# Four weights laid out transposed by the host, and rotary query weights split in attention (Trainium2, one core)

## The reference, cut to what matters

```
x  : 2048 x 512, normalised per row (xn)
q  = xn @ wq.T                  16 heads of 128 + 64 columns; rotary on the last 64
kv = xn @ wkv_a.T               128 latent columns + 64 rotary ones (rotary applied)
kv_cache = rmsnorm(kv_lat) * kv_norm_w
q_lat  = q_nope @ wkv_b[:, :128]          per head, 128 columns
scores = (q_lat . kv_cache + q_pe . k_pe) * 192**-0.5, causal, softmax
out    = ((attn @ kv_cache) @ wkv_b[:, 128:].T) @ wo.T
ffn    = xn @ ternary(w_ffn).T * mean|w_ffn| + b_ffn
result = x + out + ffn
```

## Time and profile before

| | us |
|---|---|
| median of 3 runs | 1843.85 |
| lowest and highest | 1839.24, 1846.14 |
| span of the profiled execution, first to last instruction | 1833.3 |
| preparation in it (to attention's first matmul) | 176.42 |
| busy: PE 1715.3 (94%), DVE 1211.6 (66%), POOL 1009.4 (55%), ACT 849.0 (46%) | |

### The profile page before, as it was taken

One profiled execution on the slowest core, in us unless ns is written; L12 is line 12 of the kernel. 1 busy time (PEld: TensorE's weight loads), 2 busy tenths in 40 slices (PEclk: granted clock), 3 DMA queues, 4 the chain that ended last, 5 costly groups with the idle time before them and its releaser, 6 DMA issues. The chain is left out here.

```text
span 1833.3 us, 28210 instructions
## 1 busy us (share of the span) xinstructions
PE 1715.3 (94%) x9326; PEld 1446.9 (79%) x9326; DVE 1211.6 (66%) x2801; ACT 849.0 (46%) x1358; POOL 1009.4 (55%) x635
## 2 busy tenths in 40 slices
PE   6999789888999999999999999989999999999996
PEld 5887577667777777778888888878888888888885
DVE  4765476656666776666676666767677666766763
ACT  4554344443444544444544445434544544554442
POOL 4674544443555555555556556554646555565654
PEclk9888899989999999999999999999999999999998
DMA  6995355563766656756555545565756565655553
GB/s 196 371 331 212 107 148 171 161 216 110 202 172 167 160 151 179 210 167 172 150 149 154 157 132 149 170 188 151 191 132 151 146 164 130 158 153 130 149 129 109
DMA packets 127680, 309.12 MB, mean 169 GB/s; under 512 B 29554, under 2 KB 42099, under 8 KB 126388
## 3 DMA queue, kind: packets, MB, share of 16 engines
q1 hardware_dynamic: 98784, 227.04, 43.7%
q10 hardware_dynamic: 28756, 80.35, 15.8%
HBM read 113.28 MB, written 34.60 MB: 81 GB/s over the span
## 5 line engine op out<-in xcount | busy, mean ns | idle before, releaser
L1416 POOL TENSOR_TENSOR pT<-pT,pT_h 128x1024 fp32r<-128x1024 f32 x320 | 689.3, 2184 | 415.2 <-ACT pT_h L1322 413.2
L1196 DVE TENSOR_SCALAR_CACHE_REDUCE probs<-p_score 128x512 f32<-128x512 f32 (+3 forms) x640 | 382.2, 603 | 371.7 <-PE p_score L1124 225.9
L1301 ACT ACTIVATE probs<-probs,neg_max 128x128 f32<-128x128 f32 (+15 forms) x256 | 307.6, 1202 | 449.7 <-DVE neg_max L1202 399.4
L1322 ACT ACTIVATE pT_h<-pT 128x1024 fp32r<-128x1024 f32 x320 | 291.2, 963 | 241.9 <-PE p_out L1144 175.1
L1218 DVE STREAM_TRANSPOSE turned<-probs 128x1024 f32<-128x1024 f32 (+7 forms) x384 | 341.8, 916 | 40.6 <-ACT probs L1301 36.1
L1144 PE MATMUL p_out<-pT_h,V_h 128*128 128x256 f32 (+3 forms) x1024 | 301.3, 294 | 22.7 <-POOL pT L1416 22.6
L1144 PE MATMUL p_out<-pT,V_h 128*128 128x256 f32 (+3 forms) x1024 | 303.2, 296 | 0.0
L1144 PE MATMUL p_out<-pT_h,V_l 128*128 128x256 f32 (+3 forms) x1024 | 302.8, 296 | 0.0
L1124 PE MATMUL p_score<-Kp,qp_h 128*128 128x512 f32 (+3 forms) x640 | 236.8, 370 | 16.8 <-POOL qp_l L1408 16.7
L1124 PE MATMUL p_score<-Kn_h,q_h 128*128 128x512 f32 (+3 forms) x640 | 241.2, 377 | 3.5 <-DVE q_l L1241 3.0
L1124 PE MATMUL p_score<-Kn_l,q_h 128*128 128x512 f32 (+3 forms) x640 | 234.5, 366 | 0.0
(11 more groups left out here) (135 smaller groups left out, 2348.4 us busy)
## 6 DMA issues: line engine op xcount, KB each, us to landing
pT<-turned SPq DMA_DIRECT2D x384, 128.0 KB, 3.5
Wq<-wq_scr ACTq DMA_DIRECT2D x63, 512.0 KB, 4.4
Wv<-wv_scr SPq DMA_DIRECT2D x63, 512.0 KB, 3.8
pT<-turned SPq DMA_DIRECT2D x192, 112.0 KB, 3.8
pT<-turned SPq DMA_DIRECT2D x192, 96.0 KB, 2.6
pT<-turned ACTq DMA_DIRECT2D x128, 128.0 KB, 3.9
Wp<-wp_scr SPq DMA_DIRECT2D x31, 512.0 KB, 4.8
pT<-turned SPq DMA_DIRECT2D x192, 80.0 KB, 2.8
```

The source lines that it names most:

```text
L1196: dve.tensor_scalar(probs[row % ROW_RING][:, b * CW:b * CW + width], p_score[n % SCORE_RING][:, 0:width], SCALE, LOWEST, ALU.mult, ALU.max ...
L1301: act.activation(probs[row % ROW_RING][:, 0:width], probs[row % ROW_RING][:, 0:width], ACT.Exp, bias=neg_max[p][:, i:i + 1], scale=1.0, ac ...
L1322: act.activation(high.rearrange("p r t i q -> p r t (i q)"), low.bitcast(F32).rearrange("p r t i q -> p r t (i q)"), ACT.Copy).then_inc(p_ ...
L1416: pool.tensor_tensor(low.rearrange("p r t i q -> p r t (i q)"), low.bitcast(F32).rearrange("p r t i q -> p r t (i q)"), high.bitcast(F32). ...
```

## The change

The host now hands over four weights transposed: `woT` (per head), `kvaT`, `ffnT`, and `wpT`, the rotary rows of wq for each pair of heads, reordered and transposed. In preparation, the transposes of wo, wkv_a and w_ffn, the order matmuls and the splitting and storing of rotary weights go. wo is split where it was loaded (ACT in `high_parts`, DVE in the new `low_outputs`, both inputs in SBUF). Of the four parts of `weights`, the query product moves from slot 2 to slot 0 of each head's four, with its results' copies from 2 to 1, the output product from 3 to 2. `norm(0)` on POOL goes ahead of `low_parts(0, 0)`, and x goes ahead of the other loads on SP. The ternary weights are written straight as ffnT. In attention, `wpT` is loaded raw (256 KB a pair), and ACT and POOL split it in the place right behind the split of the rotated queries (in the third chunk, in the other half of the head).

```diff
+def rotary_weights_unit(s):
+    if phase(s) == 2:
+        return 1 if closes_head(s) else None
+    return (2, 5, None, 6)[phase(s)] if opens_head(s) else None
...
@@ sync, prepare
-                sp.dma_start(wqp[ROPE * i:ROPE * (i + 1), :], wq_heads[h][NOPE:QK, :]).then_inc(s_load[i], 16)
-                sp.dma_start(wo[i][:, :, :], wo_heads[h]).then_inc(s_load[i], 16)
+                sp.dma_start(wo[i][:, :], t["woT"][h]).then_inc(s_load[i], 16)
+            sp.dma_start(x_in[:, :, :], x_chunks[NCH - 1]).then_inc(s_x, 16)
             sp.dma_start(ident[:, :], t["ident"]).then_inc(s_const, 16)
-            sp.dma_start(w_kva[:, :, :], t["wkv_a"].rearrange("(a p) i -> p a i", p=96)).then_inc(s_const, 16)
-            sp.dma_start(x_in[:, :, :], x_chunks[NCH - 1]).then_inc(s_x, 16)
+            sp.dma_start(kvaT[:, :, :], t["kvaT"]).then_inc(s_kva, 16)
...
+            sp.dma_start(keep["wp_raw"][:, :, :], t["wpT"][0]).then_inc(s_wp, 16)
...
-                    if k % 2:
-                        sp.wait_ge(s_pe_h, n + 1)
-                        sp.wait_ge(s_pe_l, n + 1)
-                        sp.dma_start(t["wp_scr"][...], Wp[:, :, :, :].bitcast(F32)).then_inc(s_wp_out, 16)
@@ gpsimd, prepare
-                pool.tensor_tensor(wqp_l[half, :], wqp[half, :], wqp_h[half, :].bitcast(F32),
-                                   ALU.subtract).then_inc(s_low, 1)
...
+            norm(0)
             low_parts(0, 0)
-            norm(0)
...
+                    if first and s == 15:
+                        pool.wait_ge(s_wp_h, 1)
+                        pool.tensor_tensor(Wp[:, 1, :, :], keep["wp_raw"][:, :, :], Wp[:, 0, :, :].bitcast(F32),
+                                           ALU.subtract)
@@ scalar, prepare
-                act.activation(wqp_h[half, :], wqp[half, :], ACT.Copy).then_inc(s_high, 1)
                 act.activation(wqn_h[i][:, :], wqn[i][:, :], ACT.Copy).then_inc(s_high, 1)
+                act.activation(woT_h[i][:, :], wo[i][:, :], ACT.Copy).then_inc(s_high, 1)
...
+            def low_outputs(c, k):
+                n, i = QB * c + k, k % 2
+                dve.wait_ge(s_high, 3 * n + 3)
+                dve.tensor_tensor(woT_l[i][:, :], wo[i][:, :], woT_h[i][:, :].bitcast(F32),
+                                  ALU.subtract).then_inc(s_woT_l, 1)
...
+                    if s % 4 == 2 and (more or s < 12):
+                        low_outputs(c, s // 4 + 1)
@@ attention
-                sp.wait_ge(rot_projected, g // 2)
-                sp.dma_start(Wp[:, :, :, :].bitcast(F32), t["wp_scr"][g % H // 2]).then_inc(wp_in, 16)
+                need(sp, wp_low, g // 2 - 1)
+                sp.dma_start(wp_raw[:, :, :], t["wpT"][g % H // 2]).then_inc(wp_in, 16)
...
-                need(pe, wp_in, 16 * (g // 2))
+                need(pe, wp_low, g // 2)
...
+            def high_rotary_weights(g):
+                act.wait_ge(wp_in, 16 * (g // 2))
+                act.wait_ge(rot_projected, g // 2)
+                act.activation(Wp[:, 0, :, :], wp_raw[:, :, :], ACT.Copy).then_inc(wp_high, 1)
...
+            def low_rotary_weights(g):
+                pool.wait_ge(wp_high, g // 2)
+                need(pool, qp_ready, issued["rotary"])
+                pool.tensor_tensor(Wp[:, 1, :, :], wp_raw[:, :, :], Wp[:, 0, :, :].bitcast(F32),
+                                   ALU.subtract).then_inc(wp_low, 1)
```

More of the change, by code:

```diff
@@ L606, in round_ @@
                         square(c, (4, 5, 7, 9).index(s))
-                    if first and s in LINEAR_SLOTS:
-                        for it in LINEAR_SLOTS[s]:
-                            copy_linear(it)
                     if s in (6, 8, 10, 11):
@@ L616, in round_ @@
                         high_parts(c, s // 4 + 1)
+                    if first and s == 15:
+                        act.wait_ge(s_wp, 16)
+                        act.activation(Wp[:, 0, :, :], keep["wp_raw"][:, :, :], ACT.Copy).then_inc(s_wp_h, 1)
             rounds(ENG.Activation, round_)
@@ L819, in weights @@
                 if part == 0:
[L821 removed]
+                    pe.wait_ge(s_low, 2 * n + 2)
                     need(pe, s_q_l, n)
[L823 to L839 removed]
                     for it in range(IT):
@@ L1390, in _ @@
         def _(pool):
-            issued = {"low": 0, "rotary": 0}
+            issued = {"low": 0, "rotary": 0, "weights": 0}
             def add_rotary(g):
@@ L1403, in low_rotary @@
                 need(pool, p_low, issued["low"])
+                need(pool, wp_low, issued["weights"])
                 need(pool, qp_ready, issued["rotary"])
@@ L1483, in constants @@
     by_chunk = lambda a: np.ascontiguousarray(a.T.reshape(P, NCH, CW).transpose(1, 0, 2))
-    order = np.zeros((2, ROPE, ROPE), np.float32)
-    for x in range(2):
-        for f in range(HALF):
-            order[:, 2 * f + x, HALF * x + f] = 1.0
     return {
@@ L1495, in constants, with transposed @@
         "sinT": by_chunk(np.concatenate([sin, -sin, sin, -sin], 1)),
+    }
+def transposed(wo, wkv_a, w_ffn, wq):
+    by_input = lambda w: np.ascontiguousarray(w.T.reshape(IT, P, -1).transpose(1, 0, 2))
+    apart = np.concatenate([np.arange(0, ROPE, 2), np.arange(1, ROPE, 2)])
+    pairs = wq.reshape(H // 2, 2, QK, D)[:, :, NOPE + apart, :].reshape(H // 2, P, D)
+    return {
+        "woT": np.ascontiguousarray(wo.T.reshape(H, VDIM, D)),
+        "kvaT": by_input(wkv_a[np.concatenate([np.arange(RANK), RANK + apart])]),
+        "ffnT": by_input(w_ffn),
+        "wpT": np.stack([by_input(w) for w in pairs]),
     }
@@ L1508 @@
     arrays["x"] = arrays["x"].reshape(S, D)
+    arrays.update(transposed(arrays.pop("wo"), arrays.pop("wkv_a"), arrays.pop("w_ffn"), arrays["wq"]))
     arrays.update(constants())
```

175 lines of the change are left out of this document (49 added, 126 removed).

## The result

| | before | after |
|---|---|---|
| median of 20 runs each, us | 1843.61 | 1850.59 |
| lowest and highest, us | 1832.57, 1849.12 | 1842.51, 1862.00 |
| profiled execution: span, mean granted clock | 1833.3, 0.976 | 1851.1, 0.967 |

The ratio of the times is 1.0036, with a 95% interval of 1.0021 to 1.0051: the change made the kernel some 7 us slower. The profiled execution of after took 1853.2 us by its own time, 2.1 more than its span. That of before, by the same measure some 1835 us, lies at the lower end of its runs. So the two traces lie 17.8 us apart where the medians lie 7 apart. I take places and causes from traces and sizes from ratios.

A forecast was written before the change was run, and what follows sets the result against it. It took PE work to bound attention, and PE work with half clock and waits, POOL's chain ending last at boundaries, the preparation. 7.5 + 5.4 + 3.5 - 1.4 = 15 us off 1833.3, with 10.5 added, gave 1829 us, range 1812 to 1842.

The forecast's parts named there:

- same: Whole kernel: no change that a measurement can tell, the limit being 0.5% or 9.2 us; chance 0.25.
- slower: Attention: POOL's subtract lands on PE's path where groups follow back to back; 31 times 1.39 us, 1871 us; chance 0.10.
- the 16.4 us in the preparation: Preparation: the gains forecast before attention's cost, 7.5 + 5.4 + 3.5 us.
- Start and round 0: Preparation's start to round 1: key projections at 25.1 and 65.0 us, 7.5 us gained, 6.0 of it at the start.
- Rounds 1 and 2: Middle preparation rounds: 3.4 us gained less 0.7 for the wo subtract, 2 x 2.7 = 5.4 us; both rounds take 35 us.
- the start of round 0 and the clock take it back: Preparation: longer waits and more half clock consume the gain, 10 us go; 1838 us, no change; chance 0.25.
- Last piece: End of preparation: without boundary and at full clock, three heads' wo and order products give 4.3 us, of which 3.5 taken.
- Port of DVE and POOL: Preparation: DVE's wo subtract, both inputs in SBUF, may hold POOL 0 to 1.4 us a round; 0.7 taken.
- Attention: All of attention: rotary weights' added copy and subtract, and halved loads, together cost 1.4 us, between -3 and +10.
- the 0.83 from which I let it decide: Attention: delay in us per pair at which POOL's subtract decides the sign, (16.4 + 9.2) / 31.
- taken back: Short name of "the start of round 0 and the clock take it back": 10 us go, 1838 us; chance 0.25.
- The base: Whole kernel: the median of 1843.85 us lies 10.5 above the profiled span, a distance left unchanged in the forecast.

The follow-up runs named there:

- e1: The changed kernel without the split of rotary weights in attention (raw weights still loaded, pair 0's split used for all pairs): 1830.55 us, 0.9946 of before.
- e7: The changed kernel plus 14 and 7 unread identity transposes on PE, ahead of waits for POOL's low query weights in preparation rounds: 1842.54 us, 0.9998 of before.
- e11: Same 14 and 7 unread transposes as e7 in the changed kernel, but behind the waits for POOL's low half: 1853.07 us, 1.0059 of before.
- e3: The changed kernel with the first chunk's rotary split moved from unit 2 to unit 0 of the even slot: 1855.23 us, 1.0065 of before.
- e5: The changed kernel with each pair's rotary split one slot earlier, in the odd slot, and raw weights loaded in the even slot: 1846.54 us, 1.0006 of before.

## Why the prediction was wrong

I forecast 1829 us, 15 off. It came out 7 above. By the 0.5% that the prediction took for the least it could tell, that is "same", to which I gave 0.25; the interval, 1.0021 to 1.0051, says slower, to which I gave 0.10. In terms of the sum: of the 16.4 us in the preparation some 10 came (by e1), and where I added 1.4 for attention it cost 17.

*Start and round 0: right, with some luck.* The key projections were forecast at 25.1 and 65.0; they came at 23.32 and 64.18. The start gained 1.8 us more than I had (the first transpose came at 15.54 us instead of 17.2, and the query product didn't wait for wqn_l), and round 0 gave 1.0 of it back, at a clock of 0.76 for 0.90. The wait of DVE for x stayed, 4.69 us for the 4.97 of the earlier trace rows.

*Rounds 1 and 2: the waits right, the clock wrong.* I had 35 us; after has 37.74 and 37.68. That the same program ran them in 34.26 and 34.23 in another execution shows that the chains do allow it. The step that failed is that the sum has no term for the clock: it takes off PE work and keeps the 0.86 of the earlier trace rows for rounds with less work in them. It went to 0.82, with a second half-clock stretch in mid-round: 0.66 over ten us instead of 1.00, so 3.4 us. That is my rival "the start of round 0 and the clock take it back", for which I had only longer waits as a cause. These came too: PE stands 3.71 and 3.99 us for wqn_l at the boundaries behind rounds 1 and 2, where it stood 1.83 and 1.85 for wqp_l. The missing work was, by e7, another cause. The Trainium skill (TensorE: Matmul & The Clock Gate, "HAM oscillation") describes the half I used, bursts that start cold behind a wait. At the boundaries this case's traces agree: after stands 3.71 us at the second of them and runs at half clock behind it. In mid-round they don't go by the wait alone: 1.75 us cost the clock in after, and 1.75 to 1.84 us did not in e7, e11 and e1.

*Last piece: wrong, in part for the same reason.* I had 3.5 us off; it is 0.86 longer, PE busy 23.95 for 25.66 us but at 0.88 for 0.98. In e7, at 1.00, it took 26.7 us (132.19 to 158.9), so 2.5 of the 4.4 us went with the clock. The other 1.9 I had over-counted, but for up to 0.9 us of the seven transposes that e7 adds there.

*Port of DVE and POOL: over-priced.* I had 0.7 us a round for it. The eight low parts of round 2 that are still there took POOL 8.54 us, for 8.25 before, most of it in the wkb_l at the boundary (1.17 for 0.91 us). On DVE's side the median of 16 woT_l subtracts is 0.691 us against a shortest of 0.673, and the longest two took 1.15 and 1.21. Beside the ternary pass POOL's wqn_l took 3.12 us at 23.07, as wqp_l did in the earlier trace rows.

*Attention: this step decided the sign.* I priced the split at what stands behind it on ACT and POOL, and found slack in both. I never asked who waits for its result: PE's projection, which in the first chunk opens the odd slot. There the 1.26 us stand behind 2.6 of qp_l, a memset of 6.97 for pair 2, or a pair of groups. I wrote "no new wait of PE for POOL"; there were seven, 15.6 us. The sentence that SP's load waits for an earlier slot's subtract, "nothing", was true and beside the point: the load's lateness is what e3 ran into.

*The rival "slower"* had the right thing, POOL's subtract on PE's path, with the wrong place and the wrong link: in the second chunk, through the groups. There PE's waits for Wp are only 4.5 us in seven. Its price, 1.39 us for each of 31, would have made 43; measured are 17, or 0.55 a pair, less than the 0.83 from which I let it decide, but against 10 us of gain instead of 16.4 it was enough for slower. A slip in another rival: "taken back" adds 10 us to 1829, which is 1839 and not 1838.

*The base.* I added the 10.5 us between span and median as if they were fixed. Spans lie 2 to 4 us below their own times; the rest is that the profiled execution lay at the lower end. The spread goes with the clock: after's runs go from 1842.5 at 0.974 to 1862.0 at 0.965. In e1's fastest execution the preparation took the 160.3 us that I had forecast, and the median of e1 shows that most executions don't.

## What to carry to other kernels

When a stored, ready-made operand is replaced by one made on the spot, follow its result to the engine that consumes it, in the stage with the shortest slots, and count the whole chain (load, first half, second half) back from there; a place where both producing engines are idle made the same work free here, within the 0.2% that the medians tell, and the kernels with three other places (after, e3, e5) are 11 to 22 us slower than the one without the split. Taking work from TensorE in a stage where it also waits can cost its clock: look at the granted clock of a stretch as at a term of the sum, and at more than one execution, since the same program ran a round in 34.2 and in 37.7 us, and the same part of attention in 231 and in 244. Where the first fix of a wait only renames it, the new name is the next thing to move.

## What the runs showed of the hardware that I had not expected

Useless matmuls can pay: 21 transposes of 0.12 us in each middle round made the kernel 0.38% faster, and the median clock of its runs rose from 0.970 to 0.977. With the 14 at the boundary on the other side of the wait the kernel was 0.61% slower than that (1.0059 for 0.9998), and no better than after (1.0036; the intervals overlap). And whether the clock falls behind a given wait is not a property of the program: with the wait at 1.84 us it stayed at 2.4 GHz in one execution, and with 1.75 us it went to 1.2 GHz in another. A 2 MB load also landed in 8.6 us in one execution and in 13.7 in another of the same attention program.
